# Spreading the rows of B over the partitions in float32 on two halves of TensorE's rows, in place of a three-part bf16 split

## The reference, cut to what matters

```python
u = silu(conv(xi) + conv_b)                       # 128 channels, 1024 positions
x_dbl = u @ W_x.T
dt = softplus(x_dbl[..., :dt_rank] @ W_dt.T + b_dt)
Bs = x_dbl[..., dt_rank:dt_rank + 16]             # 16 rows of B
Cs = x_dbl[..., dt_rank + 16:]                    # 16 rows of C
def step(h, inp):
    dt_t, B_t, C_t, u_t = inp
    dA = exp(dt_t[..., None] * A)
    h = dA * h + (dt_t * u_t)[..., None] * B_t[:, None, :]
    return h, einsum('bdn,bn->bd', h, C_t)
```

## Time and profile before

| what | us |
|---|---|
| median of three runs (761.38 to 764.2) | 761.7 |
| time of the profiled execution | 765.13 |
| its span, first to last instruction | 763.0 |
| mean granted clock of TensorE | 0.93 |

### The profile page before, as it was taken

One profiled execution on the slowest core, in us unless ns is written; L12 is line 12 of the kernel. 1 busy time (PEld: TensorE's weight loads), 2 busy tenths in 40 slices (PEclk: granted clock), 3 DMA queues, 4 the chain that ended last, 5 costly groups with the idle time before them and its releaser, 6 DMA issues.

```text
span 763.0 us, 10828 instructions
## 1 busy us (share of the span) xinstructions
PE 612.9 (80%) x3591; PEld 256.9 (34%) x3591; DVE 570.7 (75%) x589; ACT 440.5 (58%) x662; POOL 473.7 (62%) x254
## 2 busy tenths in 40 slices
PE   3876696796887777876868888988987868999994
PEld 2321121121221212211212223446663325677751
DVE  3488998998998999999989998445563435666643
ACT  1887767577578578676685752444545214555521
POOL 6359999999999999999999999500003100000001
PEclk9999789899998998997989999989999889999997
DMA  3389667576666675775666762000001110000001
GB/s 97 83 266 295 225 236 237 197 251 243 217 232 228 210 261 206 240 244 204 245 236 202 257 224 84 1 1 2 2 11 43 46 45 1 1 2 2 1 1 59
DMA packets 34009, 107.48 MB, mean 141 GB/s; under 512 B 7061, under 2 KB 7582, under 8 KB 33950
## 3 DMA queue, kind: packets, MB, share of 16 engines
q1 hardware_dynamic: 31382, 102.89, 39.8%
q10 hardware_dynamic: 1928, 2.65, 1.1%
q0 software_dynamic: 640, 1.18, 0.5%
HBM read 98.84 MB, written 4.19 MB: 135 GB/s over the span
## 4 chain that ended last, share of the span: by engine, by line
PE 41%; DVE 18%; issue 16%; POOL 12%; ACT 7%; DMA 3%; SPq 1%; DVEq 0%; POOLq 0%; ACTq 0%
DVE hh_all L1461 8%; PE py L229 6%; PE pb L198 6%; POOL hc L1759 6%; POOL dbu L1770 6%; PE px L252 5%; PE py L714 5%; DVE pb L1456 4%; PE pb L925 2%; PE px L741 2%; PE pb L702 2%; DMA cc<-scr 2%; PE px L242 1%; PE py L949 1%; DVE yg L1470 1%
## 5 line engine op out<-in xcount | busy, mean ns | idle before, releaser
L1759 POOL TENSOR_TENSOR hc<-hh_all,cc 128x1024 f32<-128x1024 f32 x128 | 302.7, 2434 | 2.8 <-DMA cc<-scr 1.4
L714 PE MATMUL py<-hc,w_cst 64*64 64x512 f32 x1024 | 157.0, 672 | 26.8 <-POOL hc L1759 18.5
L1461 DVE TENSOR_TENSOR_SCAN hh_all<-da,pb 128x1024 f32<-128x1024 f32 x72 | 164.6, 2286 | 2.5
L1773 POOL TENSOR_TENSOR yg<-w_xs 128x512 f32<-128x512 f32 x10 | 12.7, 1268 | 242.7 <-DVE w_xs L1597 153.4
L1461 DVE TENSOR_TENSOR_SCAN hh_all<-pb,dbu 128x1024 f32<-128x1024 f32 x56 | 127.7, 2280 | 17.7 <-POOL dbu L1770 14.2
L1770 POOL TENSOR_TENSOR dbu<-bb,dtu_all 128x1024 f32<-128x1024 f32 x56 | 136.3, 2434 | 0.0
L702 PE MATMUL pb<-bc,w_sel 128*128 128x512 bf16 x144 | 48.8, 424 | 64.3 <-DVE hh_all L1461 61.7
L1167 ACT ACTIVATE pb<-dt_all,w_aneg 128x1024 f32<-128x1024 f32 x56 | 62.6, 1117 | 59.0 <-DVE hh_all L1461 57.4
L1456 DVE TENSOR_TENSOR pb<-pb,dtu_all 128x1024 f32<-128x1024 f32 x72 | 87.5, 1215 | 1.8 <-DVE dtu_all L1442 0.2
L285 DVE TENSOR_REDUCE gate_all<-pb 128x1 f32<-128x1024 f32 (+7 forms) x64 | 60.4, 985 | 31.4 <-PE pb L208 16.7
L1167 ACT ACTIVATE da<-dt_all,w_aneg 128x1024 f32<-128x1024 f32 x72 | 80.5, 1137 | 0.5
(11 more groups left out here) (292 smaller groups left out, 956.5 us busy)
## 6 DMA issues: line engine op xcount, KB each, us to landing
cc<-scr SPq DMA_DIRECT2D x128, 512.0 KB, 4.3
bb<-scr SPq DMA_DIRECT2D x56, 512.0 KB, 4.7
out<-yg ACTq DMA_DIRECT2D x8, 256.0 KB, 2.1
w_xs<-hc SPq DMA_DIRECT2D x6, 256.0 KB, 4.5
w_xst<-in_x SPq DMA_DIRECT2D x2, 512.0 KB, 5.4
scr<-bcf SPq DMA_DIRECT2D x8, 128.0 KB, 4.1
w_xs<-dt_all SPq DMA_DIRECT2D x4, 256.0 KB, 5.0
w_xs<-dtu_all SPq DMA_DIRECT2D x4, 256.0 KB, 4.9
```

Of the source, the lines that this page charges most:

```text
L714: last = nc.tensor.matmul(py[part(t), half(r)], ident[part(r), part(r)], hc[u % NHC][part(r), half(t)], start=(n == 0), stop=(n == NS - 1) ...
L1461: nc.vector.tensor_tensor_scan(hh[u % NHH][:, :], decay[:, :], drive[:, :], 0.0, ALU.mult, ALU.add).then_inc(scan_done, 1)
L1759: nc.gpsimd.tensor_tensor(hc[u % NHC][:, :], hh[u % NHH][:, :], cc[u % NCC][:, :], ALU.mult).then_inc(hc_done, 1)
```

## The change

B stays float32. After pe_bc, one copy per half (act_bc) puts the 64 partitions of half h (B and C twice) into bcs: the first half of the positions on partitions 0 to 63, the second on 64 to 127. pe_b multiplies each half by a one-hot column of the constants, broadcast to 128 columns, on 64 rows of the array. The corrections, bc3, bcf, w["sel"], GpSimd's setting up of them and the copies of hi, mid and lo go. The scratch is filled from bcs in two transfers of 64 KB. The pieces from dt on move two units earlier.

```diff
         def pe_b(pe, u):
...
             if n == 0:
-                pe.wait_ge(lo_done, 2 * q + 2)
+                pe.wait_ge(bc_done, 2 * q + 2)
             atleast(pe, scan_done, u - 1)
             for h in range(2):
-                last = nc.tensor.matmul(pb[u % 2][:, half(h)], w["sel"][:, n, :], bc3[q % 2][:, half(h)], start=True, stop=True)
+                last = nc.tensor.matmul(pb[u % 2][:, half(h)], cst[part(h), SELV + n:SELV + n + 1].broadcast_to((C, 128)),
+                                        bcs[q % 2][part(h), :], start=True, stop=True)
             last.then_inc(b_full, 1)
...
-            nc.tensor.matmul(bc_at(s, h), w["wbc"][:, :], u2[s % 2][:, half(h)], start=True, stop=False,
+            nc.tensor.matmul(bc_at(s, h), w["wbc"][:, :], u2[s % 2][:, half(h)], start=True, stop=True,
                              skip_group_check=True).then_inc(px_full[h] if s else bc0_full[h], 1)
-        def pe_bc_less_hi(pe, s, h):
...
-        def pe_bc_less_mid(pe, s, h):
...
-        def act_hi(act, s, h):
...
-        def act_mid(act, s, h):
...
-        def act_lo(act, s, h):
...
+        def act_bc(act, s, h):
             if s:
+                act.wait_ge(px_full[h], full(s, BC))
+            else:
+                act.wait_ge(bc0_full[h], 1)
+            if s >= 2:
+                act.wait_ge(b_full, own_count(NS * (s - 1)))
+                act.wait_ge(scr_in, 32 * (s - 1))
+            nc.scalar.activation(bcs[s % 2][part(h), :], bc_at(s, h)[part(h), :], ACT.Copy).then_inc(bc_done, 1)
+            if s:
+                act.wait_ge(bc_done, 2 * s + h + 1)
+                act.sem_inc(px_free[h], 1)
...
# TensorE, pieces of the next sequence
-                        if n == 4:
-                            pe_bc_less_hi(pe, q + 1, h)
-                        if n == 6:
-                            pe_bc_less_mid(pe, q + 1, h)
-                        if n == 7:
+                        if n == 5:
                             pe_dt(pe, q + 1, h)
-                        if n == 10 + h:
+                        if n == 8 + h:
                             pe_dt_add(pe, q + 1, h)
...
# ScalarE
                         if n == 4:
-                            act_hi(act, q + 1, h)
-                        if n == 5:
-                            act_mid(act, q + 1, h)
-                        if n == 6:
-                            act_lo(act, q + 1, h)
-                        if n == 8 + h:
+                            act_bc(act, q + 1, h)
+                        if n == 6 + h:
                             act_dt(act, q + 1, h)
                             act_one(act, q + 1, h)
-                        if n == 10:
+                        if n == 8:
                             act_ln(act, q + 1, h)
-                        if n == 11 + h:
+                        if n == 9 + h:
                             act_dt_out(act, q + 1, h)
...
# VectorE, setup and pieces
-            for h in range(2):
-                dve_copied(dve, bcf[:, half(h)], bc_at(0, h)[0:32, :], (hi_done, h + 1), bcf_done)
-            for h in range(2):
-                dve_copied(dve, bc3[0][64:128, half(h)], bc_at(0, h)[64:128, :], (bc0_full[h], 2), mid_done)
             for h in range(2):
                 dve_zn(dve, 1, h)
-                dve_copied(dve, bc3[0][96:128, half(h)], bc_at(0, h)[96:128, :], (bc0_full[h], 3), lo_done)
...
+                        if n == 7 + h:
+                            dve_lost(dve, q + 1, h)
                         if n == 9 + h:
-                            dve_lost(dve, q + 1, h)
-                        if n == 11 + h:
                             dve_dtu(dve, q + 1, h)
...
# GpSimd, setup
-            nc.gpsimd.tensor_scalar(w["less"][:, 0, :], cst[:, IDN:IDN + 128], -1.0, None, ALU.mult).then_inc(sel_done, 1)
-            nc.gpsimd.tensor_scalar(w["less"][:, 1, 0:96], cst[:, IDN:IDN + 96], 0.0, None, ALU.mult).then_inc(sel_done, 1)
-            nc.gpsimd.tensor_scalar(w["less"][:, 1, 96:128], cst[:, IDN + 96:IDN + 128], -1.0, None, ALU.mult).then_inc(sel_done, 1)
-            nc.gpsimd.tensor_copy(w["sel"][:, :, :], cst[:, SELV:SELV + NS].unsqueeze(2).broadcast_to((128, NS, 128))).then_inc(sel_done, 1)
...
# SyncE
-            sp.dma_start(scr[s % 2, :, :], bcf[:, :]).then_inc(scr_in, 16)
+            for h in range(2):
+                sp.dma_start(scr[s % 2, :, half(h)], bcs[s % 2][C * h:C * h + 32, :]).then_inc(scr_in, 16)
```

More of the change, by code:

```diff
@@ L395, in build_all @@
         yg = [sb(f"yg_{i}", [DI, L]) for i in range(2)]
-        bc3 = [sb(f"bc3_{i}", [128, L], BF16) for i in range(2)]
-        bcf = sb("bcf", [32, L])
+        bcs = [sb(f"bcs_{i}", [128, HALF]) for i in range(2)]
         da = [sb(f"da_{i}", [DI, L]) for i in range(NDA)]
@@ L443, in outs_before @@
             return max(0, (q - 1) // 2)
-        X, GATE, BC, BHI, BMID, DT, ADD = range(1, 8)
+        X, GATE, BC, DT, ADD = range(1, 6)
         def full(s, piece):
@@ L450, in full @@
                 return {X: 1, DT: 2, ADD: 3}[piece]
-            return 3 + 7 * (s - 1) + outs_before(s - 1) + piece
+            return 3 + 5 * (s - 1) + outs_before(s - 1) + piece
         def bc_at(s, h):
             return px[h][:, :] if s else pb[1][:, h * HALF:(h + 1) * HALF]
-        def wait_bc(eng, s, h, piece):
-            if s:
-                eng.wait_ge(px_full[h], full(s, piece))
-            else:
-                eng.wait_ge(bc0_full[h], piece - GATE)
         def full_gate(q):
@@ L986, in _ @@
             for h in range(2):
[L987 to L988 removed]
                 pe_dt_add(pe, 0, h)
[L990 to L992 removed]
+            pe.wait_ge(sel_done, 1)
+            pe.wait_ge(sd_done, 4)
             pe_b(pe, 0)
@@ L1327, in _ @@
             act.preload_act_table_set("exp_and_others")
-            for piece in (act_dt, act_one, act_hi, act_ln):
+            for piece in (act_dt, act_one, act_bc, act_ln):
                 for h in range(2):
@@ L1509, in dve_lowered @@
                                     ALU.mult, ALU.add).then_inc(lo_set, 1)
-        def dve_copied(dve, to, src, ready, done):
-            dve.wait_ge(*ready)
-            nc.vector.tensor_copy(to, src).then_inc(done, 1)
         def dve_late(dve, n):
@@ L1912, in sp_scratch @@
         def sp_scratch(sp, s):
-            sp.wait_ge(bcf_done, 2 * s + 2)
+            sp.wait_ge(bc_done, 2 * s + 2)
             if s >= 2:
@@ L2011, in program @@
             w[name] = ctx.enter_context(nc.sbuf_tensor("w_" + name, shape, FP32))
-        w["sel"] = ctx.enter_context(nc.sbuf_tensor("w_sel", [128, NS, 128], BF16))
         w["less"] = ctx.enter_context(nc.sbuf_tensor("w_less", [128, 2, 128], BF16))
@@ L2035, in constants @@
     t[:, CAUS:CAUS + 128] = np.where(r[None, :] <= r[:, None], 0.0, -1e30)
-    for part in (0, 64, 96):
+    for part in (0, 64):
         t[part:part + 32, SELV:SELV + 32] = np.eye(32)
```

33 lines of the change are left out of this document (4 added, 29 removed).

## The result

**The change makes the kernel slower by 0.6%: 768.12 us (765.5 to 770.35, 10 runs) against 762.82 (761.38 to 765.85, 10 runs), ratio 1.006, 95% interval 1.0046 to 1.0074.** The forecast was 760.9, the range 758.5 to 764.5. The profiled execution took 768.86 us, with a span of 767.0 against 763.0 before. In these two profiled executions the 4.0 us have three parts: the start gives back about 2, the recurrence behind it takes 4.0 more, and the stretch behind the last hc, which I held unchanged, takes about 2 more.

A forecast was written before the change was run, and what follows sets the result against it. GpSimd was taken to bound the recurrence. A start gain of 1.1 us and a TensorE chain cost of 0.3 summed to -0.8, from the median 761.7 to 760.9 us; range 758.5 to 764.5.

The forecast's parts named there:

- What bounds the kernel: Recurrence, 66 to 475.5 us: GpSimd, busy 409.41 of 409.50 us, is the limit; savings on other engines there are worth nothing.
- the lead: Recurrence: how far the scans run ahead of GpSimd, 0.7 us at unit 3 of sequence 5; only delay beyond it costs.
- Part 1, the start: Setup before GpSimd's run: dropped casts and an earlier scratch write gain 1.1 us, bounds 0.75 and 1.4.
- First hc near 49.2, the hc after the cc wait near 64.9: Setup: sign of the start gain, the expected start times in us of these two GpSimd products.
- Part 2, the price of the spread: TensorE, recurrence: each float32 spread takes 0.96 instead of 0.54 us; four on the chain add 1.7 us.
- my own rival: TensorE spread: the halves run one after the other, b up to 1.92 us, total near 774; chance 0.06.
- Part 3, the head start of the chain: Starts of sequences 3 and 5: moved pieces let the TensorE chain begin up to 1.3 us earlier, so no cost there.
- the chain restarts late: Sequence 7: only units 2 and 3 count, 0.84 against about 0.7, a cost of 0.1 to 0.2 us.
- The term I set at 0.3: Recurrence: the total cost taken for sequences 3, 5 and 7 together, 0.3 us; 2.2 without the 1.3 head start.
- The first rival: Recurrence: TensorE takes the lead away, GpSimd idles 2 to 4 us, total 762.7 to 764.5; chance 0.15.
- The change touches nothing after the recurrence: Attention and mixture steps, from 476 us on: taken as untouched by the change.
- All three signs of being wrong: GpSimd gaps at hc of unit 3, a b over 1.05 us, or a changed length of the second half.

The follow-up runs named there:

- e7: The changed kernel with two 32 x 512 copies put back on VectorE where the setup's two casts stood; 768.37 us in one run.
- e13: The changed kernel with each float32 spread pair issued twice; 785.1 us, ratio 1.0311 to the kernel before.
- e5: The changed kernel run and profiled again, with nothing altered; 768.21 us, ratio 1.0081 to the kernel before.
- e15: The changed kernel with GpSimd's product hc of unit 124, fourth from the end, made twice; 766.95 us, ratio 1.0058 to the kernel before.
- late forms: The kernel before and the changed kernel, each with GpSimd's product hc of unit 124 made twice; 767.58 and 766.95 us.
- e4: The changed kernel with the output projection two units earlier and its ScalarE copy one unit earlier; 762.95 us, ratio 0.9999 to the kernel before.
- e8: The changed kernel with the output projection two units earlier and the eight spread transfers divided over units 4, 5 and 6; 764.44 us, ratio 1.0021 to before.
- one-pass kernels: Two runs of the changed kernel with spread operands read as bf16, one instruction per matmul; 766.52 and 769.75 us, ratios 1.0068 and 1.0084 to before.
- e1: First run of the changed kernel with the spread's operands read as bf16, one instruction per matmul; 766.52 us, ratio 1.0068 to the kernel before.

## Why the prediction was wrong

**What bounds the kernel: right.** GpSimd bounds the recurrence, and what the change delays costs what exceeds the lead.

**Part 1, the start: right in kind, 1.1 forecast, about 1.4 measured** at the hc behind the wait for cc, between means of several profiles. The casts are worth 1.7 at the first scan (1.4 forecast), but only 0.3 to 0.4 at this hc (e7), where cc decides; most of the gain there is not theirs. "First hc near 49.2, the hc after the cc wait near 64.9" came as 48.26 and 63.81.

**Part 2, the price of the spread: this step failed first.** "I take 0.96, so 0.42 more per unit": it is 1.06, so 0.52 more, since a b stands between calls of other tiles on both sides (e13). Four spreads on the chain are 2.1 us, not 1.7. I had weighed the rule of the Trainium skill ("TensorEngine Tiling (Array Packing)", Key Properties), that a change of tiling mode drains the array, at 0.1 us on one b of each chain. The runs agree with the rule and with the 0.1 us for float32 calls, but it falls on both sides of every such b, and one of these two was missing from my 0.96 four times a chain. "It decides from a b of about 1.05 us on" stands in my own rival: the measured 1.06 was past that point, though not because the halves ran in series.

**Part 3, the head start of the chain: this step failed as well, and by more.** "So the chain of part 2 also starts up to 1.3 earlier": I gave the whole of the two dtu to b of unit 15, because that b waited for the scan before. The scan did end earlier by that much: at 304.09 instead of 306.69 (304.40 and 2.29), 2.6 us, of which 1.2 are GpSimd's own and 1.4 are won. But with the scan earlier the next to bind was TensorE, with a b at half clock and L713 in front, and the b started 0.7 behind its scan, at 304.79 instead of 306.74. Measured against GpSimd, only about 0.7 of the 1.3 was won: 2.1 - 0.7 = 1.4, less the lead of 0.7, is 0.7, and 0.16 + 0.62 us is what sequence 5 lost. For sequence 7 I wrote that "the chain restarts late", at a cost of 0.1 to 0.2 us. TensorE does wait for a scan again in front of b of unit 2, for 1.85 us, but that scan is itself late, behind b of unit 0, so the delay is carried over the restart. It begins with a spread of 2.0 us and two sums of 3.7 in all at half clock:

```profile
405.69 2.08 PE L681 MATMUL pb<-bcs,w_cst 64*128 64x512 f32 x4 [3.34 <-DVE hh_all L1424]
407.70 3.69 PE L694 MATMUL py<-hc,w_cst 64*64 64x512 f32 x16
...
418.53 1.13 PE L681 MATMUL pb<-bcs,w_cst 64*128 64x512 f32 x4
419.78 1.23 DVE L1419 TENSOR_TENSOR pb<-pb,dtu_all 128x1024 f32<-128x1024 f32 x1 [1.59 <-PE pb L681]
...
423.38 1.13 PE L681 MATMUL pb<-bcs,w_cst 64*128 64x512 f32 x4 [1.85 <-DVE hh_all L1424]
...
430.15 1.29 DVE L1433 TENSOR_TENSOR yg<-py,gate_all 128x512 f32<-128x512 f32 x2 [1.20 <-PE py L694]
```

VectorE waited 1.59 for b of unit 0, y waited 1.20 for its sum, and hc of unit 3 came 1.8 us late (434.98). 0.56 followed at unit 7, where I had looked at no lead at all. How much is lost goes with the half clock at the head of the chain. In sequence 7 it is 6.8 us long in after and e5, which lose 2.4 and 2.2 us, and 3.4 in e15, which loses none; in sequences 3 and 5 it is 3.4 in after, which loses 0.9 and 0.8, and in sequence 5 of e15 it is 6.8, with 2.1 lost. The term I set at 0.3 measured 4.0, 3.8 and 2.8 (after, e5, e15), the upper end that I had given ("with a half-clock stretch there up to 3 to 4"). Start and recurrence together: -1.4 and 2.8 to 4.0, so +1.4 to +2.6, where the sum said -0.8. The first rival, "TensorE takes the lead away", was the right mechanism at 0.15, and its "2 to 4 us" held this measured size.

**"The change touches nothing after the recurrence": true of the code, not of its length.** The rear was 2.6 us longer in the profiles of after. That it goes with the way the rear is entered, and is no fixed price of the edit, is shown by e15, which has more work, a rear of 275.9 and no longer a time. If the two kernels are averaged with their late forms, the extra product taken off (762.8 and 767.6 - 2.4; 768.1 and 767.0 - 2.4), the means are 764.0 and 766.4, and by this estimate the change costs 2.4 us, which lies in what the recurrence and the start explain. It rests on four medians: unshifted the kernels are 5.3 us apart, shifted after is 0.6 below before. About half of the measured 5.3 us is then the change in the recurrence, the other half is where the half-clock spells of the rear fall. What sets them is open: in 18 profiles the rear does not go with the time at which it starts (473.0 and 476.1 give 274.3 for e4's kernel, 474.5 gives 280.7 for e8), and no experiment here held everything but the clock fixed. It was also not tried to find why one-pass kernels run so long at half clock.

All three signs of being wrong that I had named came: idle times at hc of unit 3, a b over 1.05, and another length of the second half. My chance of 0.10 for slower was too low for two terms of opposite sign each as large as the lead, of which the helpful one was entered at its upper bound.

## What to carry to other kernels

When an edit shortens the wait at the head of a chain, do not credit the whole of it: look up what the engine does just before, at the clock it has there, and credit only up to the next thing that binds. Price an instruction between the neighbours it will have, not between those of the row it is read from; here a cost of 0.1 us at a change of tiles counted on both sides, in every unit. Where the profile shows spells of half clock in a later part, 0.5% of total time can come from a shift by 2 us alone, so judge such a change by the part it touches and by a copy of both kernels that is shifted on purpose.

## What the hardware showed beside that

- A pair of float32 calls of 64x128x512 on opposite row halves takes 0.86 us among its like, a pair of bf16 ones 0.32 with one sum behind it. A change of tiles, between 64x64 and 64x128 or 128x128, adds 0.1 us to such a float32 call on either side. A pair of bf16 calls of 128x128x512 between 64x64 sums takes 0.54 us and two such pairs 0.97, so 0.11 is paid in all.
- Kernels that gave TensorE less to do in the recurrence ran it at half clock for longer (one pass: 129 and 126 us; before: 75 and 68; after: 51 and 61; the spread twice, e13: 7) and were not faster for it. Busy time alone does not tell: it is 323 us in e1 and 324 in before, 341 in after, and 376 in e13, whose recurrence is 18 us longer.
- The end of the program is not of one length either: from the last arithmetic to the end it is 7.8 to 9.5 us in 16 of the profiles, and 12.0 and 18.7 in the two one-pass ones.
